# A transformer layer on eight cores: the attention bias in two buffers and computed one block ahead, and int32-to-f32 casts folded into the subtraction that follows them

## What is computed

```
x = x + layernorm(attention(layernorm(x)))
x = x + layernorm(ffn(layernorm(x)))
attention: scores = q k^T - slope[h] * |pos_q - pos_k|, causal, softmax(scores / 8) v, then Wo
ffn: h = x w1 + b1;  h = fix(h);  h = pwl_gelu(h);  h = fix(h);  out = fix(h w2 + b2)
fix(v) = round(v * 256) / 256
pwl_gelu(v) = piecewise linear GELU with 33 breakpoints from -4 to 4 (a step of 0.25)
```

## Time and profile before

| | |
|---|---|
| median of 3 runs | 7626.43 us (7625.65 to 7635.45) |
| the profiled execution's time | 7629.88 us |
| its span (first to last instruction, core 5) | 7628.2 us |
| spans of the eight cores | 7611.8 to 7628.2 us |
| mean granted PE clock of the cores | 0.557 to 0.561 of full |

### The profile page before, as it was taken

How to read it: one execution, slowest core, us unless ns; L and a number is a source line. 1 busy time by engine, 2 the same in 40 slices (tenths; PEclk the granted TensorE clock), 3 DMA queues, 4 the chain that set the end, 5 groups by cost and what they waited for, 6 DMA issues and landing times.

```text
span 7628.2 us, 43738 instructions; the slowest of 8 cores (7611.8 to 7628.2 us)
## 1 busy us (share of the span) xinstructions
PE 2956.3 (39%) x7440; PEld 846.1 (11%) x7440; DVE 3257.9 (43%) x5129; ACT 2707.9 (35%) x3961; POOL 198.9 (3%) x372
## 2 busy tenths in 40 slices
PE   3436666654446666666211111104431111111253
PEld 1111111111111111112000000001110000000010
DVE  3332111123331111112477777772337777777423
ACT  1113444421114444410255555551115555555212
POOL 0000000000000000000000000001100000000011
PEclk7665555556665555555555555555555555555555
DMA  2110011121111111111100000002220000000132
GB/s 58 39 47 22 17 29 31 36 53 39 39 46 31 36 31 35 32 49 56 55 6 6 7 6 6 7 7 82 84 75 9 6 6 7 6 6 10 44 98 71
DMA packets 121345, 252.88 MB, mean 33 GB/s; under 512 B 14322, under 2 KB 57458, under 8 KB 121076
## 3 DMA queue, kind: packets, MB, share of 16 engines
q1 hardware_dynamic: 85748, 153.59, 6.8%
q0 software_dynamic: 29440, 77.62, 4.1%
q10 hardware_dynamic: 5888, 18.88, 0.7%
HBM read 216.47 MB, written 39.85 MB: 34 GB/s over the span
## 4 chain that ended last, share of the span: by engine, by line
DVE 37%; PE 28%; ACT 12%; issue 9%; DMA 8%; DVEq 4%; ACTq 1%; POOL 0%; SPq 0%; POOLq 0%
DVE c_et L643 11%; PE pSp L387 6%; DMA w2st<-w2bf 5%; PE pPp L431 5%; DVE c_rft L643 3%; DVEq L84 3%; PE pMp L819 3%; PE pPp L320 3%; PE pWp L546 3%; PE pCp L431 3%; PE pPp L341 3%; ACT psbt L406 2%; ACT c_at L635 2%; ACT sqscrt L189 2%; PE pZp L462 2%
## 5 line engine op out<-in xcount | busy, mean ns | idle before, releaser
L789 PE MATMUL pMp<-xlT2t,w1st 128*128 128x512 bf16 x1024 | 355.9, 524 | 2329.7 <-ACT c_ut L662 2327.5
L406 ACT ACTIVATE psbt<-pSp,biasmatt 128x512 bf16<-128x512 f32 (+3 forms) x1280 | 792.9, 625 | 1025.5 <-PE pSp L387 494.3
L635 ACT ACTIVATE c_at<-c_et,ladct 128x512 f32<-128x512 f32 x1312 | 933.2, 722 | 589.2 <-DVE c_et L730 190.5
L643 DVE SCALAR_TENSOR_TENSOR c_et<-c_at,c_et 128x512 f32<-128x512 f32 x1312 | 909.2, 693 | 329.5 <-ACT c_at L635 301.3
L387 PE MATMUL pSp<-Qsb,Ksb 64*128 64x512 bf16 (+3 forms) x1280 | 677.8, 540 | 2.0 <-DVE biasmatt L370 2.0
L819 PE MATMUL pMp<-w2st,hqt 128*128 128x512 bf16 x1024 | 442.0, 586 | 600.8 <-DMA w2st<-w2bf 255.6
L418 DVE TENSOR_TENSOR psbt<-psbt,maskst 128x128 bf16<-128x128 bf16 x512 | 115.4, 225 | 1264.3 <-ACT psbt L406 1264.3
L189 ACT ACTIVATE sqscrt<-xstaget,statst 128x1024 f32<-128x1024 f32 x112 | 129.0, 1152 | 1143.2 <-DVE statst L184 1143.2
L431 PE MATMUL pPp<-psbt,Vsb 128*65 128x512 bf16 (+3 forms) x768 | 434.7, 566 | 170.3 <-ACT psbt L406 101.2
L789 PEld LDWEIGHTS pMp<-xlT2t,w1st 128*128 128x128 bf16 x1024 | 124.8, 126 | 2560.4 <-issue 2526.7
L635 ACT ACTIVATE c_at<-c_rft,ladct 128x512 f32<-128x512 f32 x384 | 270.7, 721 | 291.4 <-DVE c_rft L686 247.0
(11 more groups left out here) (92 smaller groups left out, 3243.5 us busy)
## 6 DMA issues: line engine op xcount, KB each, us to landing
w2st<-w2bf POOLq DMA_DIRECT2D x256, 256.0 KB, 2.9
xstaget<-x_full SPq DMA_DIRECT2D x64, 512.0 KB, 3.6
wstgt<-w SPq DMA_DIRECT2D x64, 512.0 KB, 4.6
xstaget<-x_my SPq DMA_DIRECT2D x48, 512.0 KB, 3.9
xstaget<-x2scr SPq DMA_DIRECT2D x32, 512.0 KB, 4.7
w1st<-w1bf SPq DMA_DIRECT2D x64, 256.0 KB, 2.6
w1bf<-wstgbt SPq DMA_DIRECT2D x32, 256.0 KB, 2.6
w2bf<-wstgbt SPq DMA_DIRECT2D x32, 256.0 KB, 2.4
```

The lines of the kernel that those rows point to most:

```text
L406: io.activation(out=psb[PB][:, C0:512], in_=pS[PB][:, C0:512], func=AF.Exp, bias=biasmat[:, KT:KT + 1], scale=0.125), sem="s")
L635: io.activation(out=Bb[:, L:Hh], in_=V[:, L:Hh], func=AF.Sign, bias=ladc[:, CL:CL + 1], scale=1.0), sem="s")
L643: io.scalar_tensor_tensor(out=V[:, L:Hh], in0=Bb[:, L:Hh], scalar=float(-C / 2.0), in1=V[:, L:Hh], op0=ALU.mult, op1=ALU.add), sem="v")
L789: tm = op("tensor", lambda io, cc=c, HF=half, BUF=buf: io.matmul(pM[HF][:, 0:512], w1s[BUF][:, cc * 128:(cc + 1) * 128], xlT2[:, cc * 1024 ...
```

## The change

Two things are changed.

*Bias.* There are two bias tiles, used in turn by the units of a head group. The computation of a unit's bias, with its waits and its drain, becomes a function, `emit_bias`. It is called for the next unit right behind the last step of the present one: in DVE's list that is behind the last mask (L418) and ahead of the wait for the last AV matmul and the product of L442. It waits for the last exponential that read its buffer, which is that of the unit before the present one. The first unit of each head group still computes its own bias at its start. So there are 64 bias computations as before, 62 of them in a new place.

*Casts.* In three of four places where c_ti is cast to c_tf and then subtracted by a scalar_tensor_tensor, cast and subtraction become one tensor_tensor that subtracts the int32 tile c_ti from c_u. The places are L673 and L675, L728 and L730 (both 64 times) and L852 and L854 (16 times). The fourth (L684 and L686) stays.

```
+        biasmat2 = e(nc.sbuf_tensor("biasmat2t", [128, NT], F32))
...
-             "bias_free": 0,
+             "bias_free": [0, 0],
...
+            bias_bufs = [biasmat, biasmat2]
+            def emit_bias(idx):
+                h_ = hg * 8 + idx // NG
+                g_ = idx % NG
+                bsel_ = idx % 2
+                wait("vector", "s", G["bias_free"][bsel_])
+                t = op("vector", lambda io, sl=SLOPES[h_], col=h_ * NG + g_,
+                       BM=bias_bufs[bsel_]:
+                       io.tensor_scalar(
+                           out=BM[:, 0:NT], in0=kpos[:, 0:NT],
+                           scalar1=sl / 8.0, scalar2=qshift[:, col:col + 1],
+                           op0=ALU.mult, op1=ALU.add), sem="v")
+                drain("vector")
+                return t
+            pend = {}
...
-                    csel = (h8 * NG + g) % 2
+                    gidx = h8 * NG + g
+                    csel = gidx % 2
...
-                    wait("vector", "s", G["bias_free"])
-                    t_bias = op("vector", lambda io, sl=slope, col=h * NG + g: ...
-                    drain("vector")
+                    bsel = gidx % 2
+                    bmat = bias_bufs[bsel]
+                    t_bias = pend.pop(gidx, None)
+                    if t_bias is None:
+                        t_bias = emit_bias(gidx)
...
-                                       func=AF.Exp, bias=biasmat[:, KT:KT + 1],
+                                       func=AF.Exp, bias=BM[:, KT:KT + 1],
...
                         G["psb_free"][pb] = t_av
+                    G["bias_free"][bsel] = last_exp
+                    if gidx + 1 < 32:
+                        pend[gidx + 1] = emit_bias(gidx + 1)
                     t_avl = cnt["t"]
                     wait("vector", "t", t_avl)
...
-                    G["bias_free"] = last_exp
...
-            op("vector", lambda io: io.tensor_copy(out=c_tf[:], in_=c_ti[:]))
-            drain("vector")
-            op("vector", lambda io: io.scalar_tensor_tensor(
-                out=c_e[:], in0=c_tf[:], scalar=-1.0, in1=c_u[:],
-                op0=ALU.mult, op1=ALU.add), sem="v")
+            op("vector", lambda io: io.tensor_tensor(
+                out=c_e[:], in0=c_u[:], in1=c_ti[:], op=ALU.subtract), sem="v")
```

More of the change, by code:

```diff
@@ L404, in attention_group @@
                         wait("scalar", "t", G["psb_free"][pb])
-                        t_exp = op("scalar", lambda io, KT=kt, C0=c0, PB=pb:
+                        t_exp = op("scalar", lambda io, KT=kt, C0=c0, PB=pb,
+                                   BM=bmat:
                                    io.activation(
                                        out=psb[PB][:, C0:512], in_=pS[PB][:, C0:512],
-                                       func=AF.Exp, bias=biasmat[:, KT:KT + 1],
+                                       func=AF.Exp, bias=BM[:, KT:KT + 1],
                                        scale=0.125), sem="s")
```

## The result

The changed kernel takes 7394.08 us (median of 8 runs, 7382.40 to 7397.62), the kernel before 7626.07 us (median of 8, 7622.65 to 7635.45): a ratio of 0.9691, 95% interval 0.9681 to 0.9702, or 232 us less. The forecast was 7391 us, and the sum behind it 236.6 us.

The account below looks back on a forecast made before the run. No engine was busy half the span, so waiting between engines set the time. Terms 113.8 + 16.5 + 0 + 98.6 + 7.7 = 236.6 us off 7629.9 gave 7393.3; adjusted to the runs' median, 7391 us, range 7370 to 7430.

Parts of the forecast that it names:

- (a): Start of attention units g = 1 to 3: early bias starts the first exponential 2.37 us sooner, 48 times, 113.8 us.
- (b): Start of g = 0 attention units: early bias brings the first mask 1.18 us sooner, 14 times, 16.5 us.
- (c): Bias between last mask and normaliser product: hidden in DVE's free time, costing 0, at most 25 us.
- (d): Rounding chains of the first FFN matmul: 128 casts removed at 0.77 us, int32 operand at 1225 ns, 98.6 us.
- (e): Epilogues of the second FFN matmul: 10 of 16 removed casts count, at 0.77 us each, 7.7 us.
- 1 (the normaliser delayed): Rival at the unit's end: the new bias delays the normaliser, in full 25 us, 7416 us; chance 0.08.
- 2 (nothing gained at the units' start): Rival: another wait replaces the bias at units' start, only the casts are saved, 7521 us; chance 0.04.
- 3: Rival in the casts: the int32 operand costs its own pass, so the cast's saving is lost, 7497 us; chance 0.04.
- 4: Rival in the casts: mixed-type tensor_tensor runs at a fraction of the rate, at three times 7729 us; chance 0.02.
- 5 (PE's clock rises): Rival in attention: PE idles less between units and its clock rises, 230 us more saved, 7160 us; chance 0.02.
- 6 (a cast worth more than its row): Rival in the casts: each removed cast saves 1.12 us, 48 us more in all, 7343 us; chance 0.01.

Follow-up runs that it names:

- Run 7: The changed kernel with the weight casts moved from behind the units to inside those of g = 1 to 3: 7283.51 us.
- run 5: The changed kernel with each bias computed twice in a row into the same buffer: 7399.42 us.
- run 6: The changed kernel with each bias computed five times in a row into the same buffer: 7466.07 us.
- run 8: The changed kernel with the fourth cast folded too, its scalar_tensor_tensor reading the int32 tile: 7338.12 us.
- run 1: The changed kernel with the three folded casts put back, so the bias part alone: 7494.51 us, ratio 0.9829 to the kernel before.
- run 9: The changed kernel with weight casts inside units of g above 0, each head's row exponential moved, and each normaliser in five pieces inside the next unit: 7107.43 us.
- run 2: The kernel before with only the three casts folded, bias unchanged: 7516.39 us, ratio 0.9861.
- run 3: The changed kernel with both bias tiles, but each bias computed at its unit's start, behind the weight casts: 7517.06 us.
- run 4: The changed kernel with the bias in its new place but only one bias tile: 7390.28 us.

## Why the prediction was right, point by point

**(a) Bias early, g = 1 to 3: 113.8 us forecast.** The gap between the AV matmuls of two such units fell from 9.745 to 7.384 us (mean over cores and 48 units), 2.36 us each and 113.3 us in all. What made the step hold was to ask what is late next: 441.1 us stood in the groups, 131 came off.

**(b) Bias early, g = 0: 16.5 us forecast.** 15.88 to 14.65 us, 1.23 each, 17.2 us in all. Run 7 shows that the casts were the limit, by taking them away.

**(c) The new place: 0.** Right: mask to product stayed what it was, 0.97 us, in all but four of the 62 units (see the last section). The room that was said to be left, 0.34 us, was mis-sized: runs 5 and 6 show 0.22. Two errors partly cancel. The bias starts 0.14 us behind the start of the mask, not behind its end; but the waits between bias and product take 0.37 us, not the 0.16 of a single issue gap.

**(d) The chains: 98.6 us.** 97.4 measured. The price of the mixed instruction, the largest open term, is 1225 ns, the row it was taken from; run 8 shows the same for scalar_tensor_tensor. The Trainium skill, "VectorE: DVE Perf Modes", section "Specifications", says that the engine computes in f32 inside and converts integer operands. It gives no price for the conversion, and the runs show none: 1225 and 694 ns with an int32 operand, as with f32.

**(e) The epilogues: 7.7 us.** 7.6 measured as a mean over cores, but that is not clear of noise: run 1, with no cast folded, has the same two stages 4.3 us shorter than before. Shown are six of the ten: PE's six waits for wosum fell from 181.4 us (181.0 in run 1) to 176.0 as a mean over cores, 0.9 us each against 0.77 forecast. That the four epilogues of the two last pairs count and the six covered ones do not is argued and not shown.

**The rivals.** 1 (the normaliser delayed): excluded in the changed kernel by the 0.97 us, and real as soon as a second bias is added. 2 (nothing gained at the units' start): excluded by run 1. 3 and 4 (the int32 operand is dear): excluded by the 1225 ns. The argument against 4 had less under it than it said: of "both integer rows", show one, the cast, and none with two tensors. 5 (PE's clock rises): the clock stayed on its lower level, 1.2 GHz; windows over the first attention stage, core 5, of the changed kernel and then of run 9:

```profile
628.00:1570.00 942.00, 689.75 (x1342) 153.78 (x1342) 175.12 (x452) 440.61 (x710) 16.89 (x31) 0.50 0.10 28
```

```profile
625.00:1430.00 805.00, 687.64 (x1341) 153.83 (x1341) 175.77 (x453) 440.15 (x713) 16.54 (x31) 0.50 0.14 35
```

PE was busy 690 of 942 us and 688 of 805, and was granted 0.50 of full speed both times. 6 (a cast worth more than its row): the change gives 0.76 us a cast in the chains, run 2 0.79 and run 8 0.80, against the row's 0.77. By the flush of the Trainium skill, "VectorE: DVE Perf Modes", section "The DRAIN you can't avoid", a cast would be worth an estimated 1.12 us; none of the three agrees.

**Open.** The first of the two chain stages took 1366.7 to 1366.9 us with two bias tiles (the changed kernel, runs 3, 5 to 7 and 9) and 1365.2 with one (runs 2 and 4), though no bias is touched there; in the pair without folded casts it is the other way round, 1415.6 with one (before) and 1415.1 with two (run 1). No run here tells why.

## What to carry to other kernels

When a wait stands in the profile, look in the timeline at what would become ready next: the part of the idle time up to that point is the gain, and the rest only changes its name. A second buffer helps only where the buffer is what the writer waits for; here the writer stood too far back in its engine's own list, and one buffer written earlier did the same. What an in-order engine has to do between two units is better done inside them: moving the casts and the normaliser there brought another 287 us (run 9) after the 232 of the change. The casts went where DVE had nothing else to do and cost nothing; the normaliser lengthened the units by 2.2 to 3.2 us and still paid, since the gap shrank by more.

## What was not expected

DVE started the bias 0.14 us behind the start of a mask that takes 0.23 us: two of its instructions overlapped where no drain stood between them. And at the ends of units 26 and 58 the product came 1.32 to 1.34 us behind the mask in place of 0.97, and at those of units 13 and 45 1.07. It is the same four units on all eight cores, so it belongs to the program and not to chance; the kernel before has none, and run 3, with the bias at its old place, has one (unit 13, 1.32). It costs 0.9 us in all. Its cause is open.
